# One more add on GpSimd, and matmuls of zeros to open the sums' bank, in an attention kernel

## The chip, the cores and the metric

One NeuronCore of a Trainium2 chip runs the whole kernel. The metric is the device time in microseconds (us) of one execution. TensorE does matmuls, VectorE maxima and small arithmetic, ScalarE exponentials and copies, GpSimd additions and masks; SyncE (SP) issues DMAs. Each works through its own queue in order and waits on semaphores.

## The reference

A transformer block for 2 sequences of 2048 tokens with 512 channels, conditioned by a vector: adaptive layer norm, causal attention with 16 heads of 32 channels, a gated residual, adaptive layer norm, an MLP with 2048 hidden channels, a gated residual. All in f32.

```python
mod = jax.nn.silu(condition) @ Wada + bada
sh_a, sc_a, gt_a, sh_m, sc_m, gt_m = jnp.split(mod, 6, axis=1)
xn = _layernorm(x, g1, be1)
xm = xn * (1.0 + sc_a[:, None, :]) + sh_a[:, None, :]
x = x + gt_a[:, None, :] * _attention(xm, Wqkv, Wproj, bproj)
...
scores = jnp.einsum('bhqd,bhkd->bhqk', q, k) * scale
scores = jnp.where(causal, scores, -jnp.inf)
attn = jax.nn.softmax(scores, axis=-1)
out = jnp.einsum('bhqk,bhkd->bhqd', attn, v)
```

Each row of the softmax needs the sum of its exponentials. The change concerns how these sums are made.

## The kernel before

The kernel has three stages: q, k and v; attention, whose first add on GpSimd is at 336.86 us and whose last group ends near 1364 us; projection and MLP. Attention works through NG = 8 groups of GH = 4 heads. In a group the queries are taken in chunks of CH = 512, the longest first: position 0 is chunk 3, which sees 16 key tiles of 128; position 1 is chunk 2 with 12; position 2 is chunk 1 with 8; position 3 is chunk 0 with 4. That makes NS = 40 steps (position, key tile kt) in a group: 0 to 15, 16 to 27, 28 to 35, 36 to 39. The last four steps of a position lie on the diagonal; there the first `mid(s)` = 0, 128, 256 or 384 columns are left out.

A step goes through the engines like this:

- `scores` (L1453, TensorE): four matmuls, one for each head, into a ring of three banks `st`.
- `exps` (L1252, ScalarE): four exponentials into one of BUF = 5 buffers `prob`. It waits until the product that last read the buffer is done, and until GpSimd has added what it should of that buffer (`released`).
- `select` (L1191, GpSimd): on diagonal steps, the mask over the first 128 columns of the part kept.
- `product` (L1470, TensorE): four matmuls with the values into `o_ps`. They go to the four 32-row strips of the output. On a "direct" step four more matmuls with ones (L1477) put the sums of the exponentials into `r_ps`; the first direct step of a position opens that bank with `start=True`.
- `add` (L1208, GpSimd): on the other, "pooled" steps GpSimd adds the exponentials elementwise into `psum_k`; the first of them only serves as an input of the second. At the end of the position `total` (L1491, TensorE) brings `psum_k` into `r_ps` with four matmuls.

The tables `POOLED` (for groups 0 to 6) and `POOLED_LAST` (for group 7) say which key tiles of a chunk are pooled. A chunk's number is the key of the table: chunk 1 is position 2. Before the change its eight steps 28 to 35 are pooled for kt 0, 1, 2, 4, 5 and direct for kt 3, 6 and 7 (steps 31, 34 and 35).

The order on TensorE is written out: block b holds the scores of steps 2b and 2b + 1 and the products of steps 2b - 2 and 2b - 1, each product behind one step's scores; where block b - 1 ends a position, both products stand behind both steps' scores. So products 34 and 35 come after the scores of steps 36 and 37. Between the scores come matmuls for the next row maxima (`mx`, L1433), which VectorE reduces (L1309, L1313). A plan spreads them over the blocks by weights from `load`; that function looks at which steps are direct, but its term is cut at 1700, and for the pair of steps 30 and 31 it is over 1700 with step 31 direct (340 + 855 + 1710) or pooled (340 + 855 + 855), so that the plan stays as it is.

The order on GpSimd is also written out:

```python
for s in range(L.NS):
    if s in L.selects:
        select(g, s)
    if s - 1 in L.sums[more].adds:
        add(g, s - 1, more)
    if not after and 0 <= s - ONES < GH:
        key_ones(s - ONES)
```

`key_ones` (L1184, group 0 only, at steps 35 to 38) writes rows of ones into the second key buffer, and TensorE's first scores of group 1 wait for all four (`ones_ready`). `mask_row` is a bf16 row of 512 columns on each partition, zero except in a part of its last 128; the maxima on the diagonal use it.

Of the kernel before, what the change touches and what calls it, by code (L numbers as in the profile page):

```python
# [15 lines left out]
HEADS, HD = 16, 32  # L16
# [7 lines left out]
GH = P // HD  # L24
# [150 lines left out]
class Plan:  # L175


    POOLED = {3: (0, 1, 2, 3, 4, 5, 6, 8, 9, 10, 12, 13), 2: (0, 1, 2, 3, 4, 5, 6, 8, 9), 1: (0, 1, 2, 4, 5), 0: ()}
    POOLED_LAST = {3: (0, 1, 2, 4, 5, 6, 8, 9, 10, 12), 2: (0, 1, 4, 7), 1: (), 0: ()}

    def __init__(self):
# [22 lines left out]
        for pos, found in ((1, self.batch[1]), (2, self.batch[2]), (QC - 1, mixed)):  # L204
            work += [*found[:LATER], pos - 1, *found[LATER:]]
        self.sums = {True: Sums(self, self.POOLED), False: Sums(self, self.POOLED_LAST)}
        self.NA = self.sums[True].NA
# [706 lines left out]
def phase_attention(nc, K, E, L, x, wproj, bproj):  # L914
# [7 lines left out]
    with ExitStack() as ctx:  # L922
# [3 lines left out]
        def pb(name, shape):  # L926
            return ctx.enter_context(nc.psum_tensor(name, shape, F32))
# [28 lines left out]
        r_ps = pb("r_ps", [P, CH])  # L956
# [41 lines left out]
        def exp_count(g, tiles):  # L998
            return GH * L.NS * g + tiles + 1
# [7 lines left out]
        def mask_count(g, n):  # L1007
            return L.ND * g + n
# [408 lines left out]
        def tensor(pe):  # L1417
# [39 lines left out]
            def product(g, u, s, more):  # L1457
                pos, kt = L.steps[s]
                m = L.mid(s)
                end = s == L.last[pos]  # L1460
                if s == 0:
                    pe.wait_ge(v_loaded[u], 16 * (g // 2 + 1))
                if kt == 0:
                    pe.wait_ge(o_copied, QC * g + pos + 1)
                pe.wait_ge(exp_done, exp_count(g, GH * (s + 1)))
                if L.diagonal(s):
                    pe.wait_ge(masked, mask_count(g, L.selects.index(s) + 1))
                for h in range(GH):
                    rows = slice(h * HD, (h + 1) * HD)
                    ins = nc.tensor.matmul(o_ps[rows, m:], v_sb[u][:, kt, rows], prob[:, s % BUF, h, m:],  # L1470
                                           start=(kt == 0), stop=end)
                if L.sums[more].direct(s):
                    opens = L.sums[more].first_direct(s)
                    if opens:
                        pe.wait_ge(r_taken, QC * g + pos + 1)
                    for h in range(GH):
                        ins = nc.tensor.matmul(r_ps[h * HD:(h + 1) * HD, m:], K.ones[:, 0:HD], prob[:, s % BUF, h, m:],  # L1477
                                               start=opens, stop=end and not L.sums[more].added(pos))
                ins.then_inc(pv_done, 1)
                if end:  # L1480
                    total(g, s, pos, more)

            def total(g, s, pos, more):
                if not L.sums[more].added(pos):
                    pe.wait_ge(pv_done, pv_count(g, s + 1))
                    pe.sem_inc(r_ready, 1)
                    return
                n = sum(r <= s for r in L.sums[more].adds)
                pe.wait_ge(pool_added, add_count(g, n))
                for h in range(GH):  # L1490
                    ins = nc.tensor.matmul(r_ps[h * HD:(h + 1) * HD, :], K.ones[:, 0:HD], psum_k[:, pos % 2, h, :],  # L1491
                                           start=False, stop=True)
                ins.then_inc(r_ready, 1)
# [16 lines left out]
            def body(g, u, after, more):  # L1510
                for b in range(1, L.NB + 1):
                    share = None if more else L.projected(b)
                    single = more and b - 1 not in L.last_block
                    if share and b == L.NB:
                        for t in range(KT):
                            project(g, *share, t)
                    for e in range(2):
                        s = 2 * b + e

                        def between(h):  # L1520
                            stream_items(g, u, b, more, (GH * e + h,))
                            if share and h % 2 == 0:
                                project(g, *share, 2 * e + h // 2)

                        if s < L.NS:
                            scores(g, u, s, between)
                        elif more:
                            if not after:
                                pe.wait_ge(ones_ready, GH)
                            scores(g + 1, 1 - u, s - L.NS, between)  # L1530
                        if single:
                            product(g, u, s - 2, more)
                    if not single:
                        for s in (2 * b - 2, 2 * b - 1):
                            product(g, u, s, more)
# [566 lines left out]
```

## Time and profile before

| | before |
|---|---|
| median of 3 runs | 2168.27 us (2166.67 to 2168.96) |
| profiled execution, time | 2166.27 us |
| profiled execution, span of the trace | 2164.5 us |
| TensorE busy | 2126.7 us (98%) |
| VectorE busy | 1298.2 us (60%) |
| ScalarE busy | 930.0 us (43%) |
| GpSimd busy | 954.1 us (44%), x383 |
| adds of GpSimd (L1208) | 150 + 23, 4.42 and 4.58 us each |

Times within the profile are counted from the start of the span. The ends of matmuls are modelled, so starts are the surer marks. A busy share is an average over stages; GpSimd's work lies almost wholly in attention.

### The profile page before, as it was taken

What the parts mean: (1) busy time and instruction counts of PE and PEld (TensorE: products, weight loads), DVE (VectorE), ACT (ScalarE), POOL (GpSimd) and SP (SyncE); (2) the same over time, 40 slices, a digit from 0 to 9 for tenths busy, and PEclk for the clock granted to TensorE, in tenths of its full rate; (3) what the DMA queues carried; (4) which work ended last, traced back from release to release, by engine and by line L of the source; (5) the groups of instructions that cost most, each with busy time, mean ns of one, the idle gap of its engine ahead of it and who ended that gap; (6) DMA issues with size and microseconds to landing.
All of it is one profiled execution on the core that took longest, in us unless ns stands there. A gap on an engine that the chain in (4) does not pass through costs nothing.

```text
span 2164.5 us, 30729 instructions
## 1 busy us (share of the span) xinstructions
PE 2126.7 (98%) x11326; PEld 1429.4 (66%) x11326; DVE 1298.2 (60%) x2872; ACT 930.0 (43%) x1780; POOL 954.1 (44%) x383
## 2 busy tenths in 40 slices
PE   8999999999999999999999999899999999999999
PEld 7888885445444445454444544688888888888887
DVE  6878877777777777777777756794312312122122
ACT  2111115566566656656666666436322222222221
POOL 2001007989799797988979784660000000000000
PEclk9999999999999999999999999999999999999999
DMA  7548347234362523626244324684201011011010
GB/s 286 185 153 270 134 168 184 50 89 104 70 143 50 123 51 81 137 65 133 51 99 89 70 69 138 211 314 156 97 1 59 14 45 59 1 59 59 1 39 20
DMA packets 129310, 223.29 MB, mean 103 GB/s; under 512 B 8574, under 2 KB 26054, under 8 KB 128968
## 3 DMA queue, kind: packets, MB, share of 16 engines
q1 hardware_dynamic: 108568, 180.43, 30.6%
q10 hardware_dynamic: 20592, 40.90, 5.0%
q8 instruction: 90, 1.47, 0.3%
q14 instruction: 60, 0.49, 0.1%
HBM read 146.31 MB, written 74.98 MB: 102 GB/s over the span
## 4 chain that ended last, share of the span: by engine, by line
PE 80%; POOL 9%; DVE 5%; issue 3%; DMA 1%; ACT 1%; SPq 0%; POOLq 0%; DVEq 0%; ACTq 0%; PEldq 0%
PE m_hid L1973 16%; PE p_acc L1987 16%; PE acc L861 12%; PE st L1453 10%; PE mx L1433 9%; PE o_ps L1470 9%; POOL psum_k L1208 8%; PE r_ps L1477 3%; DVE part L1313 2%; PE p_acc L1952 1%; PE r_ps L1491 1%; ACT prob L1252 1%; POOL prob L1191 1%; PE misc L815 1%; PE acc L839 1%
## 5 line engine op out<-in xcount | busy, mean ns | idle before, releaser
L1252 ACT ACTIVATE prob<-st 128x512 f32<-128x512 f32 (+3 forms) x1280 | 608.8, 540 | 374.5 <-PE st L1453 361.0
L1208 POOL TENSOR_TENSOR psum_k<-psum_k,prob 128x2048 f32<-128x2048 f32 (+1 forms) x150 | 663.4, 4423 | 20.7 <-ACT prob L1252 5.8
L1313 DVE TENSOR_REDUCE part<-mx 128x1 f32<-128x512 f32 x707 | 458.0, 685 | 74.8 <-PE mx L1433 70.4
L1453 PE MATMUL st<-q_st,k_st 98*128 98x512 f32 (+3 forms) x1280 | 490.8, 395 | 4.0 <-PE r_ps L1477 1.4
L1433 PE MATMUL mx<-k_st,qx_st 96*128 96x512 f32 (+3 forms) x1196 | 442.7, 394 | 10.3 <-DVE part L1313 3.2
L1453 PEld LDWEIGHTS st<-q_st,k_st 98*128 98x128 f32 x1280 | 241.3, 189 | 267.1 <-ACT prob L1252 152.2
L1874 DVE TENSOR_TENSOR m_g_lo<-m_g,m_g_hi 128x512 fp32r<-128x512 f32 x128 | 88.6, 692 | 479.5 <-ACT m_g_hi L1791 479.3
L1433 PEld LDWEIGHTS mx<-k_st,qx_st 96*128 96x128 f32 x1196 | 223.6, 189 | 130.0 <-DVE part L1313 60.9
L1470 PE MATMUL o_ps<-prob,v_sb 128*32 128x512 f32 (+3 forms) x2560 | 297.4, 539 | 3.4 <-POOL prob L1191 3.4
L1309 DVE CUSTOM_DVE_ANT_0 unused<-mx,mask_row 128x512 bf16<-128x512 f32 (+2 forms) x489 | 228.9, 486 | 118.9 <-PE mx L1433 109.0
L1784 ACT ACTIVATE m_g<-m_hid,vcol 128x512 f32<-128x512 f32 x128 | 88.3, 689 | 471.3 <-PE m_hid L1973 471.2
L1973 PE MATMUL m_hid<-m_xm_hi,w_hi 128*128 128x512 f32 x512 | 199.6, 390 | 0.0
L1973 PE MATMUL m_hid<-m_xm_lo,w_hi 128*128 128x512 f32 x512 | 199.2, 389 | 0.0
L1987 PE MATMUL p_acc<-w_lo,m_g_hi 128*128 128x512 f32 x512 | 199.2, 389 | 0.0
L1973 PE MATMUL m_hid<-m_xm_hi,w_lo 128*128 128x512 f32 x512 | 199.2, 389 | 0.0
L1987 PE MATMUL p_acc<-w_hi,m_g_hi 128*128 128x512 f32 x512 | 199.2, 389 | 0.0
L1987 PE MATMUL p_acc<-w_hi,m_g_lo 128*128 128x512 f32 x512 | 199.2, 389 | 0.0
L1208 POOL TENSOR_TENSOR psum_k<-prob 128x2048 f32<-128x2048 f32 x23 | 105.3, 4577 | 205.8 <-ACT prob L1252 205.5
L1191 POOL TENSOR_SCALAR_AFFINE_SELECT prob<-prob 128x512 f32<-128x512 f32 x128 | 81.4, 642 | 81.0 <-ACT prob L1252 80.0
L1973 PEld LDWEIGHTS m_hid<-m_xm_lo,w_hi 128*128 128x128 f32 x512 | 96.2, 188 | 20.1
L1987 PEld LDWEIGHTS p_acc<-w_hi,m_g_hi 128*128 128x128 f32 x512 | 96.1, 188 | 20.0
L1987 PEld LDWEIGHTS p_acc<-w_hi,m_g_lo 128*128 128x128 f32 x512 | 96.1, 188 | 19.9
(186 smaller groups left out, 2535.1 us busy)
## 6 DMA issues: line engine op xcount, KB each, us to landing
k_st<-qk_scratch SPq DMA_DIRECT2D x96, 256.0 KB, 8.1
qx_st<-qk_scratch SPq DMA_DIRECT2D x96, 256.0 KB, 5.0
q_st<-qk_scratch SPq DMA_DIRECT2D x96, 256.0 KB
qk_scratch<-st_hi ACTq DMA_DIRECT2D x16, 1024.0 KB, 4.2
qk_scratch<-st_lo ACTq DMA_DIRECT2D x16, 1024.0 KB, 7.0
xs<-in_x_dram SPq DMA_DIRECT2D x8, 1024.0 KB, 9.8
v_sb<-v_scratch SPq DMA_DIRECT2D x8, 1024.0 KB, 16.4
o_scratch<-o_sb SPq DMA_DIRECT2D x32, 256.0 KB, 2.3
```

Source lines behind the costliest of these rows:

```text
L861: ins = nc.tensor.matmul(acc[j % 4][:, :], a, b, start=(t == 0 and k == 0), stop=(t == KT - 1 and k == 2))
L1191: nc.gpsimd.affine_select(out=tri, in_=tri, compare_op=ALU.is_ge, fill=0.0, base=0, pattern=[[0, GH], [1, P]], channel_multiplier=-1).then ...
L1208: nc.gpsimd.tensor_tensor(dst, src, prob[:, s % BUF, :, m:], ALU.add).then_inc(pool_added, 1)
L1252: nc.scalar.activation(prob[:, s % BUF, h, m:], st[n % RING][:, m:], ACT.Exp, scale=SCALE).then_inc(exp_done, 1)
L1309: nc.vector.tensor_tensor_reduce(spare[:, 0:w], bank[:, 0:w], K.mask_row[:, CH - w:], 1.0, LOWEST, ALU.add, ALU.max, most).then_inc(mx_fre ...
L1313: nc.vector.tensor_reduce(most, bank[:, 0:w], AX.X, ALU.max).then_inc(mx_free, 1)
L1433: nc.tensor.matmul(out[:, 0:w], qx_st[n % 3][0:ROWS, h, t * P:(t + 1) * P], k_st[u][0:ROWS, h, kc * CH:kc * CH + w], start=True, stop=True ...
L1453: nc.tensor.matmul(st[n % RING][:, m:], k_st[u][0:MROWS, h, kt * P:(kt + 1) * P], q_st[0:MROWS, pos % 2, h, m:], start=True, stop=True).th ...
L1470: ins = nc.tensor.matmul(o_ps[rows, m:], v_sb[u][:, kt, rows], prob[:, s % BUF, h, m:], start=(kt == 0), stop=end)
L1874: nc.vector.tensor_tensor(g_lo[:, j % 4, :], g32[:, j % 2, :], raw(g_hi[:, j % 4, :]), ALU.subtract).then_inc(g_ready, 1)
L1973: ins = nc.tensor.matmul(hid[j % HB][:, :], a, b, start=(t == 0 and k == 0), stop=(t == KT - 1 and k == 2))
L1987: ins = nc.tensor.matmul(acc[s][:, :], a, b, start=(j == 0 and k == 0), stop=(j == HT - 1 and k == 2))
```

## The change

Step 31 (kt 3 of the eight-step chunk) becomes pooled in groups 0 to 6. The first direct step of that position is then step 34, which covers only columns 256 to 511. So that all of the bank is opened, four matmuls of zeros, one for each head's strip, with `start=True` write columns 0 to 255 ahead of it; the step's own matmuls then no longer open. The group's adds go from 23 to 24. Nothing else of the kernel is changed.

```diff
-    POOLED = {3: (...), 2: (...), 1: (0, 1, 2, 4, 5), 0: ()}
+    POOLED = {3: (...), 2: (...), 1: (0, 1, 2, 3, 4, 5), 0: ()}
...
                     if opens:
                         pe.wait_ge(r_taken, QC * g + pos + 1)
+                    if opens and m:
+                        for h in range(GH):
+                            nc.tensor.matmul(r_ps[h * HD:(h + 1) * HD, 0:m], K.mask_row[:, 0:HD], K.mask_row[:, 0:m], start=True, stop=False)
                     for h in range(GH):
                         ins = nc.tensor.matmul(r_ps[h * HD:(h + 1) * HD, m:], K.ones[:, 0:HD], prob[:, s % BUF, h, m:],
-                                               start=opens, stop=end and not L.sums[more].added(pos))
+                                               start=opens and not m, stop=end and not L.sums[more].added(pos))
```

## Rows read from the trace of the kernel before

**Rows 1.** The page: chain that ended last, shares by engine.

```profile
PE 80%; POOL 9%; DVE 5%; issue 3%; DMA 1%; ACT 1%; SPq 0%; POOLq 0%; DVEq 0%; ACTq 0%; PEldq 0%
```

**Rows 2.** GpSimd's timeline, group 3, position 2: start, length, idle before in brackets.

```profile
826.41 0.63 POOL L1191 TENSOR_SCALAR_AFFINE_SELECT prob<-prob 128x512 f32<-128x512 f32 x1 [1.15 <-ACT prob L1252]
829.13 0.63 POOL L1191 TENSOR_SCALAR_AFFINE_SELECT prob<-prob 128x512 f32<-128x512 f32 x1 [2.09 <-ACT prob L1252]
829.74 4.55 POOL L1208 TENSOR_TENSOR psum_k<-psum_k,prob 128x2048 f32<-128x2048 f32 x1
834.24 0.63 POOL L1191 TENSOR_SCALAR_AFFINE_SELECT prob<-prob 128x512 f32<-128x512 f32 x1
834.84 3.48 POOL L1208 TENSOR_TENSOR psum_k<-psum_k,prob 128x1536 f32<-128x1536 f32 x1
838.28 1.37 POOL L1191 TENSOR_SCALAR_AFFINE_SELECT prob<-prob 128x512 f32<-128x512 f32 x2
```

**Rows 3.** TensorE's timeline, group 3, positions 2 and 3.

```profile
829.71 1.04 PE L1477 MATMUL r_ps<-prob,ones 128*32 128x512 f32 x8
830.68 0.38 PE L1453 MATMUL st<-q_st,k_st 98*128 98x256 f32 x1
...
835.39 0.85 PE L1470 MATMUL o_ps<-prob,v_sb 128*32 128x384 f32 x8
...
840.14 0.64 PE L1470 MATMUL o_ps<-prob,v_sb 128*32 128x256 f32 x8
840.60 0.61 PE L1477 MATMUL r_ps<-prob,ones 128*32 128x256 f32 x8
841.03 0.40 PE L1470 MATMUL o_ps<-prob,v_sb 128*32 128x128 f32 x8
841.25 0.40 PE L1477 MATMUL r_ps<-prob,ones 128*32 128x128 f32 x8
...
842.44 0.39 PE L1453 MATMUL st<-q_st,k_st 98*128 98x256 f32 x1
```

**Rows 4.** ScalarE's timeline: last exponentials of step 32, those of steps 36 and 37.

```profile
825.64 0.60 ACT L1252 ACTIVATE prob<-st 128x512 f32<-128x512 f32 x1 [0.18 <-PE st L1453]
...
836.79 3.95 ACT L1252 ACTIVATE prob<-st 128x512 f32<-128x512 f32 x8 [1.59 <-PE st L1453]
```

**Rows 5.** VectorE's timeline, group 3.

```profile
831.30 0.29 DVE L1309 CUSTOM_DVE_ANT_0 unused<-mx,mask_row 128x128 bf16<-128x128 f32 x1 [0.91 <-PE mx L1433]
...
846.31 0.56 DVE L1309 CUSTOM_DVE_ANT_0 unused<-mx,mask_row 128x384 bf16<-128x384 f32 x1 [1.49 <-PE mx L1433]
```

**Rows 6.** GpSimd's timeline over attention: group 0's memsets; group 4 opens; select 15.

```profile
450.78 0.63 POOL L1191 TENSOR_SCALAR_AFFINE_SELECT prob<-prob 128x512 f32<-128x512 f32 x1
451.47 1.80 POOL L1184 MEMSET k_st<- 2x2048 f32 x1
453.46 0.63 POOL L1191 TENSOR_SCALAR_AFFINE_SELECT prob<-prob 128x512 f32<-128x512 f32 x1 [0.19 <-POOL k_st L1184]
...
459.52 1.80 POOL L1184 MEMSET k_st<- 2x2048 f32 x1
...
853.39 4.58 POOL L1208 TENSOR_TENSOR psum_k<-prob 128x2048 f32<-128x2048 f32 x1 [5.59 <-ACT prob L1252]
...
905.41 0.66 POOL L1191 TENSOR_SCALAR_AFFINE_SELECT prob<-prob 128x512 f32<-128x512 f32 x1
```

**Rows 7.** TensorE's timeline at the end of position 0, group 4.

```profile
906.22 0.42 PE L1470 MATMUL o_ps<-prob,v_sb 128*32 128x128 f32 x8 [0.26 <-POOL prob L1191]
...
907.66 0.50 PE L1453 MATMUL st<-q_st,k_st 98*128 98x512 f32 x1
```

**Rows 8.** TensorE's timeline at the end of group 0.

```profile
459.74 0.83 PE L1477 MATMUL r_ps<-prob,ones 128*32 128x384 f32 x8
461.38 0.50 PE L1453 MATMUL st<-q_st,k_st 98*128 98x512 f32 x1 [0.81 <-POOL k_st L1184]
```

**Rows 9.** TensorE's timeline in the projection.

```profile
1407.02 1.06 PE L1960 MATMUL p_tp<-ident,k_whole 128*128 128x128 f32 x8 [3.30 <-DVE k_whole L1865]
```

**Rows 10.** Windows there: PE, PEld, DVE, ACT, POOL busy; granted clock; DMA share, GB/s.

```profile
1408.00:1410.00 2.00, 2.00 (x6) 1.54 (x6) 2.00 (x5) 1.20 (x2) 2.00 (x3) 0.50 0.87 228
...
1411.00:1412.00 1.00, 1.00 (x5) 0.81 (x4) 0.97 (x6) 0.00 (x0) 0.95 (x1) 0.80 1.00 387
```

More of the change, by code:

```diff
@@ L175 @@
 class Plan:
-    POOLED = {3: (0, 1, 2, 3, 4, 5, 6, 8, 9, 10, 12, 13), 2: (0, 1, 2, 3, 4, 5, 6, 8, 9), 1: (0, 1, 2, 4, 5), 0: ()}
+    POOLED = {3: (0, 1, 2, 3, 4, 5, 6, 8, 9, 10, 12, 13), 2: (0, 1, 2, 3, 4, 5, 6, 8, 9), 1: (0, 1, 2, 3, 4, 5), 0: ()}
     POOLED_LAST = {3: (0, 1, 2, 4, 5, 6, 8, 9, 10, 12), 2: (0, 1, 4, 7), 1: (), 0: ()}
```

## The prediction

> **What bounds the kernel now.** I read the page first. The chain that ended last is 80% TensorE and 9% GpSimd [rows 1], so an edit that moves work from the one to the other can pay on either side, and the question is which of them ends the waits where the work is moved. So I read, in group 3, GpSimd's timeline around the third chunk (position 2, steps 28 to 35) [rows 2], TensorE's over the same time [rows 3], then ScalarE's and VectorE's for what feeds them [rows 4, 5], and lastly the two places where the same handover already goes wrong: the end of position 0 [rows 6, 7] and the end of group 0 [rows 6, 8].
>
> The reader is to see this. At the end of position 2 TensorE is the one that works without a gap: products 34 and 35, sums and total follow each other from 840.14 to 842.44 [rows 3]. GpSimd is behind ScalarE but has air: it was idle 1.15 us before the select of step 32 and 2.09 us before that of step 33 [rows 2]. It finishes the select of step 35 at 838.9, and product 35 starts at 841.03 [rows 3], so it is 2.1 us early. From the first add of group 4 at 853.39 on [rows 6] GpSimd runs without a gap and leads until product 15 at 906.22, which did wait 0.26 us for a select [rows 7]. So from 842.4 to 853.4 whatever TensorE loses or wins is carried to the first add of the next group, and GpSimd's own work after that is rigid. This repeats in each group.
>
> **The change, part by part.** It acts in the seven groups before the last; the last takes its lists from another table.
>
> 1. Removed: the four sums matmuls of step 31, 829.71 to the next scores at 830.68 [rows 3]. A full pipelined set moves what follows by four times the 0.215 us that a 128-column set takes (0.22 in 841.03 to 841.25, doubled to 0.43 in 840.60 to 841.03 [rows 3]), so 0.86 us. VectorE doesn't hold it back: it had been idle 0.91 us before the maximum at 831.30, waiting for TensorE [rows 5]. So TensorE would come to product 35 at 841.03 - 0.86 = 840.17.
>
> 2. Added on TensorE: four matmuls of zeros, 256 columns, bf16, in product 34. The trace shows none of this type. Bounds: nothing, if they slip into the pipeline, and 0.43 us, the time of the 256-column set in f32 [rows 3]. I take 0.2, in the middle, since nothing in the trace says which end is nearer; neither end changes the sum. TensorE is then ready for product 35 at 840.4 (840.2 to 840.6). Its wait for the sums' bank, formerly at step 31, falls 10 us later and finds the bank long read.
>
> 3. Added on GpSimd: the add of step 31, 128x2048. In program order it stands behind the select of step 32 (select first, then the add of the step before). So it can't use the idle time ahead of that select: it starts after it, at 827.02. From there GpSimd's rows chain. Start to start a select takes 0.61, a full add followed by a select 4.50 (829.74 to 834.24), a 1536 add 3.44 (834.84 to 838.28) [rows 2]. The inputs are there: exponentials of step 32 ended at 826.24 [rows 4]. So: select 32 at 826.41, add 31 827.02, select 33 831.52, add 32 832.13, select 34 836.63, add 33 837.24, select 35 840.68, done at 841.31. Before, select 35 started at 838.28: 2.40 us later now, that is 4.50 for the new add less the 2.09 of idle time that it fills.
>
> 4. Who waits for GpSimd now. Product 33 wants its mask at 835.39 - 0.86 = 834.5, has it at 832.2. Product 34 wants it at 839.3, has it at 837.3. Exponentials of step 36 (836.79 before [rows 4], now from 835.9) need add 31, done at 831.6. Those of 38 need add 33, done 840.7, and aren't asked for before 842. Product 35 wants its mask at 840.4 and gets it at 841.31. This one fails. At the end of position 0 a select that ended at 906.07 let product 15 start at 906.22, 0.15 later, and the next scores followed 1.44 after that (907.66) [rows 6, 7]; the same three sets stand here. So: product 35 at 841.46, next scores at 842.90, against 842.44 before [rows 3]. **+0.46 us per group**, and the 0.66 that TensorE had saved is spent waiting. Queued behind product 35 are the total, the scores of steps 38 and 39 and of the next group, and with them the maxima on VectorE, which had waited 1.49 us for TensorE before 846.31 [rows 5] and so shifts with it. Nothing there absorbs 0.46. The copy of the sums and of o_ps shifts too and was not late.
>
> 5. Group 0 is another matter. There GpSimd also fills the ones of the second key buffer, four memsets of 1.80 us between the selects of steps 35 to 39, back to back from 450.78 on; the last starts at 459.52 [rows 6]. TensorE, in front of group 1's first scores, waited 0.81 us for it and started at 461.38 [rows 8]. With select 35 2.40 later the whole string is later by the same: the only idle times in it are waits of 0.19 for GpSimd itself. So TensorE starts at 463.74 to 463.78: **+2.4 us once**, in place of the 0.46.
>
> Sum: 6 x 0.46 + 2.4 = 2.8 + 2.4 = +5.2 us. The profiled execution took 2166.27 (span 2164.5): 2171.5. The median of the three runs is 2.0 above it, 2168.27, and the forecast on its scale is 2173.4, +0.24%. What a measurement tells from no change here is about 0.2%, 4.3 us; so this stands just beyond it.
>
> Bounds of the sum: the 0.46 rests on eight durations that vary by 0.03 each from row to row, so 0.3 to 0.6 a group, and 2.3 to 2.5 for group 0: +4.1 to +6.1.
>
> **A rule against it.** A full add takes 4.55 us in this chunk, and 4.58 at the head of the next group [rows 2, 6], with VectorE working beside it. The Trainium skill (GPSIMD Engine Reference, Engine selection) says that an elementwise add of two tensors belongs on VectorE and is about twice as slow on GpSimd; it gives 4497 ns for one of this size. By that figure the handover would fail by some 0.3 us instead of 0.46, and the sum would be about 4. Taken as a plain warning, that GpSimd's time is the kernel's time, it gives the third rival below.
>
> **The rivals.**
>
> *The masks come in time.* What decides is whether select 35 ends by 840.3 rather than 841.3. If the new add displaced 1 us less than the rows say, TensorE's 0.66 would be kept in six groups, -4.0, and group 0 would lose about 1.4: -2.6, 2165.7. Against it: all seven groups show the same adds and the same idle times, and the add cannot be shorter than its twins. 8%. For a gain over 0.2% the ones of group 0 would have to stay in time too.
>
> *The clock falls in group 0.* TensorE would stand still from about 461.0 (459.74 + 0.83 + 0.46 [rows 8]) to 463.74, 2.7 us. Late in the kernel it stood still 3.30 us before 1407.02 [rows 9], and from 1408 to about 1411.4 the granted clock was 0.50, the 1.2 GHz level [rows 10]: 1.7 us lost. A gap of 2.7 is shorter, and no gap of that size is there to show which way it goes. +1.7 once: 2175.1. 10%.
>
> *GpSimd's time is paid in full*: 7 x 4.7 = +33, 2201. Against it the idle times in [rows 2] and the 5.6 us ahead of 853.39 [rows 6]. 2%.
>
> *A longer stall*: TensorE's items and VectorE's maxima fall into a worse step after product 35 and lose as much again, 1 us a group: +8.6, 2177. VectorE's idle 1.49 speaks against it. 7%.
>
> *No net change*: losses in the groups hidden by something that I don't see, 3%. The forecast itself has 70%.
>
> **How the numbers follow.** The forecast's own range, 4.1 to 6.1, plus 1 us for the median, straddles 4.3: about two thirds of its 70% lie beyond, 0.46. With the clock (0.10), the longer stall (0.07) and the rule (0.02): slower 0.65. Within 0.2%: the other third (0.24), the masks in time and no net change (0.08 of their 0.11): 0.32. Faster 0.03. The range runs from no net change, 2168, to the longer stall, 2177.5.
>
> **What would show it.** GpSimd: an add of 128x2048 at 0.61 behind select 32, no idle time before select 33, 180 adds in all and not 173. TensorE: a wait of about 1 us for GpSimd's select ahead of product 35 in groups 1 to 6, next scores 0.4 to 0.5 later against select 32; in group 0 a wait of 2.7 for the memset. Period of groups 1 to 6 up by 0.46, first add of group 1 later by 2.4. Wrong if the wait at product 35 is missing, if select 35 starts less than 13 us behind select 32, or if the zeros take over 1 us.

## The result and the profile after

| | before | after |
|---|---|---|
| median | 2167.40 us (7 runs, 2164.91 to 2168.96) | 2173.26 us (7 runs, 2171.49 to 2176.99) |
| profiled execution, time | 2166.27 us | 2171.49 us |
| span of its trace | 2164.5 us | 2169.7 us |

The ratio is 1.003, 95% interval 1.0021 to 1.004: slower by 5.9 us in the medians and by 5.2 us between the two profiled executions. The forecast was 2173.4, +5.2 on a median of 2168.27 from three executions; the seven beside the changed kernel have 2167.40.

The page of the changed kernel, busy time and share, then the chain that ended last (as [rows 1]) and the group of GpSimd's adds (line, busy, mean ns, idle before):

```profile
PE 2123.4 (98%) x11298; PEld 1427.1 (66%) x11298; DVE 1293.8 (60%) x2872; ACT 929.9 (43%) x1780; POOL 985.1 (45%) x390
...
PE 78%; POOL 10%; DVE 6%; issue 3%; DMA 1%; ACT 1%; SPq 0%; POOLq 0%; DVEq 0%; ACTq 0%; PEldq 0%
...
L1208 POOL TENSOR_TENSOR psum_k<-psum_k,prob 128x2048 f32<-128x2048 f32 (+1 forms) x157 | 695.4, 4429 | 20.7 <-ACT prob L1252 5.8
```

Seven adds more (157 and 23, before 150 and 23), 31 us more of GpSimd, 3.3 us less of TensorE, and the kernel is 5 us slower. GpSimd's timeline in group 3, position 2, answers to [rows 2]:

```profile
829.15 0.64 POOL L1191 TENSOR_SCALAR_AFFINE_SELECT prob<-prob 128x512 f32<-128x512 f32 x1 [1.17 <-ACT prob L1252]
829.76 4.58 POOL L1208 TENSOR_TENSOR psum_k<-psum_k,prob 128x2048 f32<-128x2048 f32 x1
834.29 0.63 POOL L1191 TENSOR_SCALAR_AFFINE_SELECT prob<-prob 128x512 f32<-128x512 f32 x1
834.90 4.57 POOL L1208 TENSOR_TENSOR psum_k<-psum_k,prob 128x2048 f32<-128x2048 f32 x1
839.42 0.63 POOL L1191 TENSOR_SCALAR_AFFINE_SELECT prob<-prob 128x512 f32<-128x512 f32 x1
840.02 3.47 POOL L1208 TENSOR_TENSOR psum_k<-psum_k,prob 128x1536 f32<-128x1536 f32 x1
843.45 1.80 POOL L1191 TENSOR_SCALAR_AFFINE_SELECT prob<-prob 128x512 f32<-128x512 f32 x3
```

The 1.17 us of idle time ahead of select 32 are still there, the 2.09 ahead of select 33 are filled by the new add, and select 35 starts 14.30 us behind select 32 (11.87 before). TensorE's timeline at the same place, to be laid beside [rows 3]:

```profile
842.01 0.64 PE L1470 MATMUL o_ps<-prob,v_sb 128*32 128x256 f32 x8
842.47 0.29 PE L1478 MATMUL r_ps<-mask_row 128*32 128x256 bf16 x4
842.58 0.61 PE L1480 MATMUL r_ps<-prob,ones 128*32 128x256 f32 x8
844.22 0.42 PE L1470 MATMUL o_ps<-prob,v_sb 128*32 128x128 f32 x8 [1.03 <-POOL prob L1191]
...
845.65 0.38 PE L1453 MATMUL st<-q_st,k_st 98*128 98x256 f32 x1
```

The zeros take 0.11 us (842.47 to 842.58). Then TensorE stands for 1.03 us until the mask of step 35 is there; the next scores come 16.50 us behind select 32 where they came 16.03 behind it before. The end of group 0, GpSimd's timeline and then TensorE's (as [rows 6, 8]):

```profile
461.64 1.80 POOL L1184 MEMSET k_st<- 2x2048 f32 x1
```

```profile
463.50 0.50 PE L1453 MATMUL st<-q_st,k_st 98*128 98x512 f32 x1 [2.73 <-POOL k_st L1184]
```

And TensorE's waits for GpSimd's masks and ones over the whole execution (engine and line, for whom: us in total, times, longest):

```profile
PE o_ps L1470 <- POOL prob L1191: 10.4, 14, 1.0
...
PE st L1453 <- POOL k_st L1184: 2.7, 1, 2.7
```

The first of them was 3.4 us in 7 waits before. Cut into stretches by the first add of each group on GpSimd, the profiled executions of all kernels of this study look like this (us, worked out from their timelines; the last column is where windows of 10 us within attention had a granted clock of at most 0.90; a low clock ahead of attention or behind it is not in it):

| kernel | to first add | group 0 | groups 1 to 6 | rest | span | clock low at |
|---|---|---|---|---|---|---|
| before | 336.86 | 129.31 | 774.06 | 924.27 | 2164.5 | |
| after | 336.56 | 131.75 | 776.93 | 924.46 | 2169.7 | 1330 |
| changed_again | 338.56 | 131.76 | 776.89 | 926.49 | 2173.7 | 1330 |
| tensor_part | 336.71 | 133.58 | 770.84 | 925.77 | 2166.9 | 380, 460, 470, 1330 |
| gpsimd_part | 338.24 | 131.81 | 776.87 | 926.18 | 2173.1 | 1330 |
| add_first | 338.42 | 132.17 | 770.73 | 924.58 | 2165.9 | 460 |
| ones_split | 338.62 | 129.57 | 776.93 | 924.68 | 2169.8 | |
| masks_in_time | 337.15 | 131.44 | 769.69 | 926.32 | 2164.6 | 380, 1320 |
| masks_in_time_everywhere | 336.76 | 128.43 | 766.97 | 926.54 | 2158.7 | 1320 |
| old_table_in_time | 337.36 | 128.57 | 771.46 | 923.91 | 2161.3 | |
| one_memset_more | 338.48 | 136.13 | 777.38 | 923.21 | 2175.2 | 460, 470 |
| zeros_eightfold | 336.56 | 133.66 | 777.90 | 924.78 | 2172.9 | 380, 460, 1330 |

Before to after: +2.44 in group 0, +2.87 in groups 1 to 6 (0.48 each), -0.1 in all the rest. The column of groups 1 to 6 is the quietest measure here; "to first add" and "rest", which no edit here touches but for two memsets, move by up to 2 and 3.3 us from execution to execution, and the medians with them.

The granted clock goes with most of that. All traces but one have stretches of 3.4 us or more at 0.50, the 1.2 GHz level (falls in the last 1.5 us of a trace left aside). Near 41 us five profiles have one (changed_again, gpsimd_part, add_first, ones_split, one_memset_more), and in these five the first add comes at 338.2 to 338.6; in the other seven it comes at 336.6 to 337.4. Within "rest" such stretches lie near 1330 and near 1410: none where it is 923.2 to 924.6, one where it is 924.3 to 925.8, two where it is 926.2 to 926.5. The profile of before has its one at 1408 [rows 10], that of after has none there and one at 1333 (windows, columns as in [rows 10]):

```profile
1331.00:1333.00 2.00, 2.00 (x5) 0.78 (x5) 1.97 (x5) 2.00 (x5) 0.00 (x0) 1.00 0.00 0
1333.00:1336.50 3.50, 3.50 (x17) 0.88 (x21) 2.72 (x5) 3.36 (x7) 1.60 (x2) 0.52 0.77 230
```

So the two profiles compared above have one low stretch each and none in groups 0 to 6; that they are so alike is luck.

### The profile page after: what moved, and what is told of

Same layout as the page of the kernel before. It is cut to its first block, busy times and chain, and to the rows that moved or that the text cites. A ratio compares the mean times of both kernels' runs of the same rounds, so it can differ in the third digit from the quotient of the medians.

```text
span 2169.7 us, 30687 instructions
## 1 busy us (share of the span) xinstructions
PE 2123.4 (98%) x11298; PEld 1427.1 (66%) x11298; DVE 1293.8 (60%) x2872; ACT 929.9 (43%) x1780; POOL 985.1 (45%) x390
## 4 chain that ended last, share of the span: by engine, by line
PE 78%; POOL 10%; DVE 6%; issue 3%; DMA 1%; ACT 1%; SPq 0%; POOLq 0%; DVEq 0%; ACTq 0%; PEldq 0%
PE m_hid L1976 16%; PE p_acc L1990 16%; PE acc L861 12%; POOL psum_k L1208 9%; PE st L1453 9%; PE mx L1433 8%; PE o_ps L1470 8%; DVE part L1313 3%; PE r_ps L1480 2%; PE p_acc L1955 2%; PE r_ps L1494 1%; ACT prob L1252 1%; POOL prob L1191 1%; PE misc L815 1%; DVE unused L1309 1%
## 5 line engine op out<-in xcount | busy, mean ns | idle before, releaser
L1208 POOL TENSOR_TENSOR psum_k<-psum_k,prob 128x2048 f32<-128x2048 f32 (+1 forms) x157 | 695.4, 4429 | 20.7 <-ACT prob L1252 5.8
L1433 PE MATMUL mx<-k_st,qx_st 96*128 96x512 f32 (+3 forms) x1196 | 443.0, 395 | 10.2 <-DVE part L1313 2.4
L1470 PEld LDWEIGHTS o_ps<-prob,v_sb 128*32 128x32 f32 x2560 | 54.3, 108 | 91.9 <-ACT prob L1252 44.6
L1990 PEld LDWEIGHTS p_acc<-w_lo,m_g_hi 128*128 128x128 f32 x512 | 96.2, 188 | 20.0
L1976 PEld LDWEIGHTS m_hid<-m_xm_hi,w_lo 128*128 128x128 f32 x512 | 96.2, 188 | 19.9
```

The source lines that it names most:

```text
L1208: nc.gpsimd.tensor_tensor(dst, src, prob[:, s % BUF, :, m:], ALU.add).then_inc(pool_added, 1)
L1433: nc.tensor.matmul(out[:, 0:w], qx_st[n % 3][0:ROWS, h, t * P:(t + 1) * P], k_st[u][0:ROWS, h, kc * CH:kc * CH + w], start=True, stop=True ...
L1976: ins = nc.tensor.matmul(hid[j % HB][:, :], a, b, start=(t == 0 and k == 0), stop=(t == KT - 1 and k == 2))
L1990: ins = nc.tensor.matmul(acc[s][:, :], a, b, start=(j == 0 and k == 0), stop=(j == HT - 1 and k == 2))
```

## The experiments

The medians of before that they are compared with lie between 2167.06 and 2167.69 us.

**tensor_part**, TensorE's half alone:

```diff
-            if kt not in chosen:
+            if kt not in chosen or (plan.order[pos], kt) == (1, 3):
```

> TensorE's part of the change alone: in groups 0 to 6 step 31 is neither summed by TensorE nor added by GpSimd (its share is left out of the row sums), and the zeros open the bank. My theory: TensorE keeps what the matmuls cost less the zeros, 0.86 - 0.11 = 0.75 us in groups 1 to 6, and nothing in group 0, where the ones set the start of group 1: -4.5 us against the kernel before, first scores after the total at 15.3 us behind the select of step 32 (16.03 before). Rival, the matmuls of step 31 were hidden (by VectorE's maxima or by the ones): between 0 and -1 us.

Measured: 2166.68 us, ratio 0.9995 (0.9986 to 1.0004). The total is a miss: -0.4 where I had -4.5. The groups say what I expected of them: from group 2 on the period is 128.19 to 128.52 where it was 128.91 to 129.28, 0.73 less on the mean, and the scores after the total come 15.27 us behind select 32 (GpSimd's timeline, then TensorE's):

```profile
830.29 0.64 POOL L1191 TENSOR_SCALAR_AFFINE_SELECT prob<-prob 128x512 f32<-128x512 f32 x1 [1.14 <-ACT prob L1252]
```

```profile
845.56 0.39 PE L1453 MATMUL st<-q_st,k_st 98*128 98x256 f32 x1
```

What gave it back in the profiled execution is group 0: 133.58, 4.3 us more than before, with the clock fallen twice. TensorE's timeline there, the first row with its idle time, and windows of the same stretch (busy time of PE, PEld, DVE, ACT, POOL, then the granted clock):

```profile
379.79 1.52 PE L1470 MATMUL o_ps<-prob,v_sb 128*32 128x512 f32 x8 [0.78 <-POOL prob L1191]
```

```profile
370.00:380.00 10.00, 8.89 (x53) 4.44 (x56) 7.72 (x16) 5.39 (x12) 9.86 (x4) 1.00 0.41 94
380.00:385.00 5.00, 5.00 (x25) 2.39 (x17) 2.96 (x9) 1.11 (x4) 5.00 (x3) 0.53 0.06 8
385.00:390.00 5.00, 5.00 (x19) 3.60 (x12) 2.52 (x6) 2.64 (x5) 4.35 (x3) 0.50 0.67 157
```

The ten executions of this kernel range from 2162.86 to 2168.75, and they go by their mean granted clock: the fastest has 0.999, the two slowest 0.994 and 0.995. Beside executions of before with the same mean, this kernel is 4.3 to 4.4 us faster (table at the end of this section). So the local saving is shown, and what the total lost goes with the clock.

**gpsimd_part**, the other half alone:

```diff
-        return kt not in self.pooled[self.plan.order[pos]]
+        return kt not in self.pooled[self.plan.order[pos]] or (self.pooled is Plan.POOLED and s == 31)
```

> GpSimd's part alone: step 31 is added by GpSimd and still summed by TensorE, which opens the bank with it as before (the step counts twice in the row sums, no zeros). My theory: product 35 waits for its mask as in the changed kernel, so taking the matmuls away was worth nothing there: +5.3 us against the kernel before, like the changed kernel, with a wait of about 0.3 us at product 35 where the changed kernel has 1.0. Rival, that the two costs add up: +5.3 + 7 x 0.75 = +10.5 us.

Measured: 2174.64 us, ratio 1.0036 (1.0024 to 1.0048): +7.6 where I had +5.3. Groups 1 to 6 take 776.87 (after: 776.93), group 0 131.81 (131.75); what this profile has on top lies ahead of attention and behind it, where the clock was low near 41, 1335 and 1417 us. TensorE's timeline at product 35:

```profile
845.91 0.43 PE L1470 MATMUL o_ps<-prob,v_sb 128*32 128x128 f32 x8 [0.26 <-POOL prob L1191]
```

It comes later by the matmuls of step 31 and waits 0.26 in place of 1.03. The matmuls taken away were worth nothing in the changed kernel: the end of the wait is set by GpSimd. The rival that adds the costs (+10.5) is out.

**zeros_eightfold**, the suspected cost of the zeros times eight:

```diff
-                        for h in range(GH):
-                            nc.tensor.matmul(..., start=True, stop=False)
+                        for r in range(8):
+                            for h in range(GH):
+                                nc.tensor.matmul(..., start=(r == 0), stop=False)
```

> The changed kernel with the four matmuls of zeros done eight times over in each group. One set takes 0.11 us in the trace of the changed kernel, so eight take 0.9, and TensorE had 1.03 us to wait for its mask at product 35. My theory: the wait at product 35 shrinks to about 0.3 us and nothing else moves: as the changed kernel, +5.3 us against the kernel before, period of groups 1 to 6 129.4 to 129.5 us. Rival, that the zeros lie on the path: +5.3 + 7 x 0.77 = +10.7.

Measured: 2173.36 us, ratio 1.0026 (1.0015 to 1.0037). TensorE's timeline in group 3:

```profile
845.44 1.06 PE L1479 MATMUL r_ps<-mask_row 128*32 128x256 bf16 x32
846.32 0.61 PE L1481 MATMUL r_ps<-prob,ones 128*32 128x256 f32 x8
847.18 0.43 PE L1470 MATMUL o_ps<-prob,v_sb 128*32 128x128 f32 x8 [0.25 <-POOL prob L1191]
```

The total is +5.7 (+5.3 expected). Eight sets take 0.88 us and the wait shrinks to 0.25. The periods of groups 2 to 6 are 129.38 to 129.69, as in the changed kernel (129.42 to 129.74); the period of group 1 is longer (130.51), because a low clock of 7 us reached into it.

**add_first**, the same work in another order:

```diff
+                    early = more and s == 32
+                    if early:
+                        add(g, s - 1, more)
                     if s in L.selects:
                         select(g, s)
-                    if s - 1 in L.sums[more].adds:
+                    if s - 1 in L.sums[more].adds and not early:
                         add(g, s - 1, more)
```

> The changed kernel, with the add of step 31 ahead of the select of step 32 in GpSimd's order, so that it uses the 1.15 us of idle time there. My theory: select 35 starts 1.4 us later than in the kernel before in place of 2.4, ends 10.5 us behind where select 32 would have run before, and product 35 starts 0.2 us after TensorE is ready: -0.5 us in each of groups 1 to 6, +1.4 us in group 0 for the ones: -1.7 us against the kernel before. Rival, that the added length of GpSimd's work is what costs and not where it stands: +5.3 as the changed kernel.

Measured: 2167.62 us, ratio 1.0005 (0.9996 to 1.0014). The total is a miss, +0.6 where I had -1.7. Groups 1 to 6 take 770.73 us, 3.33 less than before and 6.2 less than the changed kernel with the same instructions. In group 3 (GpSimd's timeline, then TensorE's) select 35 ends at 843.28 and product 35 starts at 843.42, 0.17 later than the 0.43 us of the set before it ask for; I had expected 0.2:

```profile
842.65 1.80 POOL L1191 TENSOR_SCALAR_AFFINE_SELECT prob<-prob 128x512 f32<-128x512 f32 x3
```

```profile
842.82 0.61 PE L1483 MATMUL r_ps<-prob,ones 128*32 128x256 f32 x8
843.42 0.43 PE L1473 MATMUL o_ps<-prob,v_sb 128*32 128x128 f32 x8
```

In group 0 select 35 is 23.74 us behind the chunk's first add (22.36 before), the 1.4 expected; but the group took 132.17, 1.5 more than that gives. TensorE's timeline shows why, and windows of it:

```profile
464.41 0.69 PE L1456 MATMUL st<-q_st,k_st 98*128 98x512 f32 x1 [2.73 <-POOL k_st L1184]
464.89 0.63 PE L1436 MATMUL mx<-k_st,qx_st 96*128 96x512 f32 x1
465.32 0.63 PE L1456 MATMUL st<-q_st,k_st 98*128 98x512 f32 x1
```

```profile
460.00:464.00 4.00, 1.67 (x19) 0.52 (x17) 2.72 (x6) 0.52 (x3) 3.75 (x3) 1.00 0.08 27
464.00:466.00 2.00, 1.59 (x4) 1.31 (x5) 0.44 (x1) 0.61 (x2) 0.99 (x2) 0.64 0.23 86
466.00:468.00 2.00, 2.00 (x6) 1.52 (x6) 1.64 (x4) 1.49 (x3) 0.00 (x0) 0.51 0.00 0
468.00:470.00 2.00, 2.00 (x16) 1.27 (x18) 1.88 (x5) 1.85 (x5) 0.00 (x0) 1.00 0.00 0
```

Behind a stand-still of 2.73 us the granted clock was at 1.2 GHz, and matmuls started 0.43 us apart in place of 0.23.

**ones_split**, group 0 alone:

```diff
+            for h in range(2):
+                key_ones(h)
             def body(g, u, after, more):
...
-                    if not after and 0 <= s - ONES < GH:
-                        key_ones(s - ONES)
+                    if not after and 0 <= s - ONES < GH - 2:
+                        key_ones(s - ONES + 2)
```

Within `key_ones` the waits of GpSimd on its own earlier work are dropped for the first two and stay for the others.

> The changed kernel, with two of the four memsets of ones before the first add of group 0, where GpSimd is idle, and the other two behind the selects of steps 35 and 36. My theory: group 0 no longer waits for the ones; the kernel before did too by 0.9 us, so group 0 comes to -0.4 us and groups 1 to 6 keep their +0.47: +2.4 us against the kernel before. If the stand-still of 2.7 us in group 0 is what lets the clock fall in some executions, the granted clock is nearer to 0.999 than the 0.998 of most executions of the changed kernel. Rival, that group 0 costs no more than the others: +5.3 less 0.8.

Measured: 2170.32 us, ratio 1.0015 (1.0007 to 1.0024): +3.3 where I had +2.4, and 3 us below the changed kernel. Groups 1 to 6 are unmoved (776.93). Group 0 takes 129.57: 2.2 less than in the changed kernel, but 0.26 over before where I had 0.4 below. The error is in what the ones cost before: TensorE's idle time of 0.81 [rows 8] was not all lost. Group 0 had taken only 0.3 us more than the others (129.31 against 129.0), since the first add of group 1 came 4.79 us behind the late scores where it comes 5.38 behind the first scores of other groups, which took up 0.6. What sets the pace there isn't shown. The eleven executions have a mean granted clock of 0.998 to 1.000, the twelve of the changed kernel 0.996 to 0.999, as expected if the stand-still in group 0 is one place where the clock falls.

**one_memset_more**, the stand-still longer:

```diff
-                nc.gpsimd.memset(raw(k_st[1][ROWS:MROWS, h, :]), 1.0).then_inc(ones_ready, 1)
-                pool.wait_ge(ones_ready, h + 1)
+                for r in range(1 + (h == GH - 1)):
+                    nc.gpsimd.memset(raw(k_st[1][ROWS:MROWS, h, :]), 1.0).then_inc(ones_ready, 1)
+                    pool.wait_ge(ones_ready, h + r + 1)
...
-                                pe.wait_ge(ones_ready, GH)
+                                pe.wait_ge(ones_ready, GH + 1)
```

> The changed kernel with the last memset of ones done twice in group 0, so that TensorE stands still for 4.7 us there in place of 2.7. Without any effect of the clock: +2.0 us on the changed kernel, +7.3 against the kernel before. My theory: the granted clock falls to 0.50 behind the stand-still in the profiled execution, 3.4 us long, and costs 1.7 more: +9.0. Rival: the clock stays at 1.00 there.

Measured: 2175.96 us, ratio 1.0038 (1.0024 to 1.0052), +8.9. Group 0 takes 136.13, 4.4 more than in the changed kernel for 1.9 us of stand-still more; 2.5 are the clock's. TensorE's timeline and windows:

```profile
467.34 0.79 PE L1454 MATMUL st<-q_st,k_st 98*128 98x512 f32 x1 [4.60 <-POOL k_st L1185]
```

```profile
464.00:466.00 2.00, 0.00 (x0) 0.00 (x0) 0.00 (x0) 0.00 (x0) 1.94 (x2) 0.72 0.34 131
466.00:468.00 2.00, 0.66 (x2) 0.56 (x3) 0.00 (x0) 0.00 (x0) 1.81 (x2) 0.50 0.00 0
...
474.00:476.00 2.00, 1.94 (x32) 0.89 (x28) 0.20 (x1) 0.53 (x1) 1.39 (x1) 0.72 0.00 0
```

The clock fell while TensorE still stood, and stayed low for about 10 us, not the 3.4 us that I had put at 1.7. That the total comes near the +9.0 expected is luck in part: in the profile group 0 is 6.8 over before and groups 1 to 6 are 3.3, together 10.1.

**changed_again**, for the clock:

> The changed kernel once more, unaltered, beside the kernel before: +5.3 us by the steps, and up to two falls of the clock more, 1.7 us each. The profiled execution shows whether the clock falls behind the stand-still of 2.7 us in group 0; it did in the profile of add_first and did not in the first profile of the changed kernel, so I give it even chances.

Measured: 2175.51 us (2173.46 to 2177.13), ratio 1.0036 (1.0022 to 1.005), +7.8. In its profile the clock did not fall behind the 2.73 us. With the profiles of after, gpsimd_part (no fall) and of add_first and zeros_eightfold (a fall) that makes two in five.

**masks_in_time, masks_in_time_everywhere and old_table_in_time.** The first joins add_first and ones_split and puts the select of step 35 ahead of the add of step 33; the second does this for steps 15 and 27 too; the third does the same with the table of before, where there is no add of step 31 to move. The loop of the second, without its lines for the ones, which are as in ones_split:

```diff
+                    early = more and s == 32
+                    if early:
+                        add(g, s - 1, more)
-                    if s in L.selects:
+                    if s in L.selects and not (more and s - 1 in (14, 26, 34)):
                         select(g, s)
+                    if more and s in (14, 26, 34):
+                        select(g, s + 1)
-                    if s - 1 in L.sums[more].adds:
+                    if s - 1 in L.sums[more].adds and not early:
                         add(g, s - 1, more)
```

> The changed kernel with three moves on GpSimd: the add of step 31 ahead of the select of step 32, the select of step 35 ahead of the add of step 33, and two of the four memsets of ones before the first add of group 0. My theory: no product waits for a mask at the end of position 2, so TensorE keeps its 0.75 us in each of seven groups, and group 0 loses the 0.3 us of the ones too: -5.5 us against the kernel before, period of groups 1 to 6 at 128.2 us (129.0 before). Rival, that something else of the step (VectorE's maxima, ScalarE's buffers) stands right behind the mask: -3.3 us as in add_first's groups 1 to 6, or less.

> As masks_in_time, and at the ends of positions 0 and 1 too the select of the last step (15 and 27) goes ahead of the add of the 1536 columns. My theory: the wait of product 15 for its select goes as well, 0.26 us in groups 1 to 6 and up to 0.95 in group 0: -5.5 - 2.5 = -8.0 us against the kernel before. Rival, that the later end of the add only moves the wait to the total of position 0: -5.5.

> The kernel before (step 31 summed by TensorE, no zeros), with the selects of steps 15, 27 and 35 ahead of the adds and the memsets split, as in masks_in_time_everywhere. My theory: only the waits at product 15 and for the ones go: -2.8 us against the kernel before, so that the change, with its masks in time, is worth -5.2 us on top. Rival, that the order alone made the gain of masks_in_time_everywhere: as much as that kernel, -8.

Measured: masks_in_time 2163.50 us, ratio 0.9982 (0.9973 to 0.9991), -3.6 where I had -5.5; masks_in_time_everywhere 2160.19, 0.9965 (0.9953 to 0.9978), -6.9 for -8.0; old_table_in_time 2163.42, 0.9984 (0.9975 to 0.9993), -3.6 for -2.8. GpSimd's and TensorE's timelines of the second in group 3, to be laid beside those of after:

```profile
826.14 1.22 POOL L1192 TENSOR_SCALAR_AFFINE_SELECT prob<-prob 128x512 f32<-128x512 f32 x2
827.33 4.56 POOL L1209 TENSOR_TENSOR psum_k<-psum_k,prob 128x2048 f32<-128x2048 f32 x1
831.84 1.23 POOL L1192 TENSOR_SCALAR_AFFINE_SELECT prob<-prob 128x512 f32<-128x512 f32 x2
833.03 3.48 POOL L1209 TENSOR_TENSOR psum_k<-psum_k,prob 128x1536 f32<-128x1536 f32 x1
```

```profile
835.92 0.61 PE L1489 MATMUL r_ps<-prob,ones 128*32 128x256 f32 x8
836.35 0.40 PE L1479 MATMUL o_ps<-prob,v_sb 128*32 128x128 f32 x8
...
837.76 0.39 PE L1462 MATMUL st<-q_st,k_st 98*128 98x256 f32 x1
```

The mask of step 35 is done at 833.07 and product 35 follows at 836.35 with no wait. In groups 1 to 6 masks_in_time gains 4.37 us on before (0.73 each, expected 0.75), masks_in_time_everywhere 7.09, old_table_in_time 2.60. The difference of the last two is the change with its masks in time: -4.49, six times 0.75. The rival that the order alone makes the gain is out. The medians say -3.2; I had expected -5.2. Group 0 gave 0.14 of its 0.75, and the rest of the program, which both have in common, took 2.6 us more in the one profiled execution (clock low near 1320 and 1402) than in the other (no fall). masks_in_time missed its total for a cause like tensor_part's: 131.44 in group 0 with a low clock from 380 on. masks_in_time_everywhere is the fastest kernel of the study, 6.9 us below before.

**All executions at the same granted clock.** The record has the mean granted clock of each execution, to 0.001, which is 2.2 us of time, so that a single execution says little. Against the 61 executions of before that ran beside the experiments (0.997 to 1.000), the mean times of those that had 0.998 and of those that had 0.999 differ by (us, number of executions in brackets):

| kernel | executions, clock | medians | at 0.998 | at 0.999 | expected |
|---|---|---|---|---|---|
| after and changed_again | 12, 0.996 to 0.999 | +5.9, +7.8 | +5.5 (7) | +4.2 (1) | +5.2 |
| tensor_part | 10, 0.994 to 0.999 | -0.4 | -4.3 (2) | -4.4 (1) | -4.5 |
| gpsimd_part | 6, 0.996 to 0.999 | +7.6 | +6.2 (3) | +5.3 (1) | +5.3 |
| add_first | 11, 0.994 to 0.999 | +0.6 | -0.9 (3) | -2.2 (3) | -1.7 |
| ones_split | 11, 0.998 to 1.000 | +3.3 | +2.8 (5) | +2.9 (4) | +2.4 |
| masks_in_time | 11, 0.996 to 0.999 | -3.6 | -4.5 (6) | -5.8 (3) | -5.5 |
| masks_in_time_everywhere | 5, 0.997 to 0.999 | -6.9 | -8.3 (3) | -7.7 (1) | -8.0 |
| old_table_in_time | 11, 0.996 to 1.000 | -3.6 | -2.2 (1) | -3.3 (4) | -2.8 |
| one_memset_more | 4, 0.997 to 0.998 | +8.9 | +7.3 (3) | | +9.0, 1.7 of it the clock's |
| zeros_eightfold | 7, 0.997 to 0.999 | +5.7 | | +4.3 (3) | +5.3 |

The kernels whose totals missed come near what their steps had given. The clock is also a part of what the change costs: the twelve executions of the changed kernel average 0.9974 and are 7.4 us slower than the 61 of before, which average 0.9990; 5.3 are the steps of groups 0 to 6, and some 2 us go with the lower clock. Why it is lower there isn't shown in full. The stand-still in group 0 is one place, but masks_in_time, which has none, is low as well (0.9980).

## Why the prediction was right

It was right in direction, size and mechanism, by its own steps:

1. *Removed, 0.86 on TensorE*: shown by tensor_part (0.73 a group net of the zeros) and by the last two kernels (0.75).
2. *Zeros, estimated 0.2, between 0 and 0.43*: 0.11. Neither end changed the sum, as said; zeros_eightfold shows it up to 0.88.
3. *The add stands behind the select of step 32 and select 35 moves by 2.40*: 14.27 us behind select 32 forecast, 14.30 measured. add_first shows that the place in the queue and not the amount decides: the same adds one place earlier turn +2.87 into -3.33 in groups 1 to 6.
4. *Product 35 waits, +0.46 a group*: 0.47 in group 3 (16.50 less 16.03), 0.48 on the mean; gpsimd_part shows that the mask alone sets it.
5. *Group 0, +2.4 once*: +2.44, and TensorE stood for 2.73 us (2.7 forecast). ones_split takes 2.2 of it away.

Not seen in full was the clock. As a rival it had 10% and 1.7 us for group 0, and it was no rival but comes on top in some executions: the fall came in two of five profiles with that stand-still, and falls elsewhere (near 41, near 380, near 1330, in the projection) come and go too. The median moved by 5.9 us and not by the 5.2 of the profiled pair, and the twelve executions of the changed kernel go by their mean granted clock: 2171.49 at 0.999, 2173.14 to 2175.51 at 0.998, 2176.92 to 2177.13 at 0.996. Where in an execution the clock was low is known for the two profiles alone, and both had no fall in group 0. That the median of 2173.26 lies within 0.2 us of the 2173.4 forecast is luck in part: the base was 0.9 us higher than the seven executions of before gave, and the falls made it up.

On the rule weighed in the prediction: the Trainium skill (GPSIMD Engine Reference, Engine selection) puts such adds on VectorE, and its section Elementwise — side-by-side cycle accounting has 4497 ns for an add of this size. The trace agrees on the price, 4.57 us, but the verdict does not hold for this kernel: with its masks in time the same add on GpSimd paid 0.75 us a group, since GpSimd had idle time there that no other engine waited on.

## What to carry to other kernels

When work is moved onto an engine with idle time, look where in its queue it will stand: an idle stretch that lies ahead of a wait earlier in the queue can't be used by an instruction behind that wait. Follow the queue from there to the next short instruction that a busier engine waits for (here a mask of 0.63 us behind 13.7 us of adds and other masks) and put that one ahead. A once-only piece of work that shares the queue (here the ones of group 0) can cost nearly as much as the six repetitions together (2.44 and 2.87 us).

## What the runs showed of the hardware

- A stand-still of TensorE of 2.7 us sometimes brought the 1.2 GHz clock behind it (in group 0 in two of five profiles) and one of 4.6 us did it in the one profile; the low clock lasted 3.4 to 10.2 us. In tensor_part it fell behind one of 1.6 us. In the projection all twelve profiles have such a stand-still: the clock fell behind it in four of the ten where it is 2.65 to 2.85 us long, and in both where it is 3.30.
- The clock also fell behind much shorter waits. All twelve profiles have a wait of 0.71 to 0.82 us near 380 us; in three of them (tensor_part, masks_in_time and zeros_eightfold) the clock fell there, in one for 3.4 us and in two for 10.2. In seven profiles it fell near 1330, where TensorE's longest wait in the 9 us before was 0.52 us. What sets these apart from the others isn't shown.
- Four bf16 matmuls of 256 columns to four 32-row strips take 0.11 us together; four f32 ones of the same size take 0.43.
